# A new calendar for a fused cross-attention and gated self-attention kernel: 119 stretches of 32-column products in place of 144

## What is computed

```
h = x + Wo1 · softmax(q k^T / sqrt(32), 77 context keys, masked) v      # q from layernorm(x), k and v from the context
out = h + svd_moe_o( softmax(q k^T) v )                                 # q, k, v = svd_moe(layernorm(h)), 512 keys
svd_moe(x): x @ Wm + sum over 2 chosen of 8 experts of gate * ((x @ V^T) * S) @ U^T + b
gates: softmax of the top 2 of a small two-layer net on the mean over tokens
```

## Time and profile before

| | us |
|---|---|
| runs | 1422.53, 1434.18, 1422.72 |
| median of the runs | 1422.72 |
| span of the profiled execution, first to last instruction | 1426.7 |
| TensorE busy in it | 1391.0 (97 %) |
| VectorE busy | 951.9 (67 %) |
| ScalarE busy | 861.3 (60 %) |
| GpSimd busy | 679.8 (48 %) |

### The profile page before, as it was taken

The page is one execution under the profiler, slowest core; times in us unless marked ns, Lnnn a source line. Parts: engine busy times, 40 slices in busy tenths (PEclk is TensorE's granted clock), DMA queues, the critical chain, the costliest instruction groups (busy, mean ns, idle before and its releaser), DMA issues.

```text
span 1426.7 us, 17122 instructions
## 1 busy us (share of the span) xinstructions
PE 1391.0 (97%) x5704; PEld 702.4 (49%) x5704; DVE 951.9 (67%) x1687; ACT 861.3 (60%) x1499; POOL 679.8 (48%) x411
## 2 busy tenths in 40 slices
...
PEclk9889999999999999999999999999999999999999
...
GB/s 252 143 53 133 46 68 96 153 76 46 98 110 108 75 54 125 137 61 76 68 111 123 75 59 135 110 85 67 58 104 152 76 46 97 64 101 79 81 39 30
DMA packets 78767, 130.81 MB, mean 92 GB/s; under 512 B 26374, under 2 KB 32134, under 8 KB 75607
## 3 DMA queue, kind: packets, MB, share of 16 engines
...
...
## 4 chain that ended last, share of the span: by engine, by line
PE 85%; ACT 7%; issue 2%; DMA 2%; POOL 2%; DVE 1%; ACTq 0%; SPq 0%; POOLq 0%
PE pj L1217 43%; PE scT L1302 9%; PE sc L1274 8%; PE acc L1331 7%; PE sc L1263 4%; PE pj L1247 2%; PE pj L1311 2%; PE scT L1295 2%; PE pj L1319 2%; PE pj L1340 2%; DMA qs<-shift 2%; PE pj L1190 1%; ACT xhat L810 1%; PE pj L1202 1%; PE pj L1211 1%
## 5 line engine op out<-in xcount | busy, mean ns | idle before, releaser
L925 ACT ACTIVATE probs<-scT 128x512 f32<-128x512 f32 x512 | 288.9, 594 | 303.9 <-PE scT L1302 300.8
L1048 DVE TENSOR_REDUCE negmax<-sc 128x1 f32<-128x512 f32 x512 | 338.0, 684 | 140.7 <-PE sc L1274 139.7
L784 POOL TENSOR_TENSOR probs_sum<-probs_sum,probs 128x1024 f32<-128x1024 f32 x128 | 300.2, 2365 | 57.4 <-ACT probs L925 57.3
L1075 DVE RECIPROCAL inv_sum<-pj 128x128 f32<-128x128 f32 x256 | 225.0, 921 | 59.9 <-PE pj L1340 39.2
L1274 PE MATMUL sc<-ks,qs 96*128 96x512 f32 x512 | 260.1, 541 | 2.4 <-DVE negmax L1048 1.6
L1217 PE MATMUL pj<-XT,Wqk 128*128 128x512 f32 x512 | 257.3, 598 | 0.6 <-DVE Wqk L1140 0.6
L1302 PE MATMUL scT<-qs,ks 99*128 99x512 f32 x512 | 250.9, 517 | 6.2 <-DMA qs<-shift 3.2
L780 POOL TENSOR_TENSOR probs_sum<-probs 128x1024 f32<-128x1024 f32 x64 | 151.4, 2372 | 173.8 <-ACT probs L925 173.8
L790 POOL TENSOR_TENSOR uv_stack<-UVS_sb,uv_stack 96x1024 fp32r<-96x1024 f32 x32 | 75.7, 2367 | 178.1 <-ACT UVS_sb L832 178.1
L1302 PEld LDWEIGHTS scT<-qs,ks 99*128 99x128 f32 x512 | 94.7, 191 | 124.5 <-ACT probs L925 60.4
L754 POOL TENSOR_TENSOR xhat<-xhat,inv_sum 128x128 f32<-128x128 f32 (+1 forms) x56 | 45.1, 806 | 207.7 <-DVE inv_sum L1075 207.7
...
## 6 DMA issues: line engine op xcount, KB each, us to landing
Wqk<-in_WmT SPq DMA_DIRECT2D x16, 1024.0 KB, 6.1
Wvo<-in_WmT SPq DMA_DIRECT2D x16, 1024.0 KB, 6.5
...
X<-in_x SPq DMA_DIRECT2D x8, 1024.0 KB, 6.0
ks<-stage_lo SPq DMA_DIRECT2D x128, 64.0 KB, 2.0
...
```

The costliest lines, as they stand in the source:

```text
L784: nc.gpsimd.tensor_tensor(probs_sum[:, pair], probs_sum[:, pair], probs[:, kt % 2, pair], ALU.add)\
L925: nc.scalar.activation(probs[:, kt % 2, jj, :], scT[:, ST[step], :], ACT.Exp, scale=SCALE)\
L1048: nc.vector.tensor_reduce(negmax[:, 0, n:n + 1], sc[:, SC[step], :], AX.X, ALU.max, negate=True)\
L1075: nc.vector.reciprocal(inv_sum[:, INV[use], at], pj[:, PJ[left_in(full)], at])\
```

## The change

Only the tables change. `PERIOD` goes from 2034 to 32544, which is 16 times 2034, a finer unit for the same period; every number of `CALENDAR` and `OWN` is another. No function changes, the instructions and their sizes are the same ones, and only their order differs. All lines behind the tables stand 23 further down. Two of the lines:

```
-PERIOD = 2034
+PERIOD = 32544
...
-    "normalize": (-1775, 138),
-    "xpose": (-1734, -1732, -1712, -1710, 141, 141, 163, 163),
+    "normalize": (-28358, 2045),
+    "xpose": (-27732, -27691, -27388, -27376, 2393, 2424, 3016, 3035),
```

More of the change, by code:

```diff
@@ L37 @@
 JUNK = 8
-PERIOD = 2034
+PERIOD = 32544
 CALENDAR = {
[L45 to L49, removed]
-    "normalize": (-1775, 138),
-    "xpose": (-1734, -1732, -1712, -1710, 141, 141, 163, 163),
[L52 to L84, removed]
[4 rows of a table removed]
-    "shift": (1339, 1901, 2375, 2899),
-    "shift_move": (1367, 1967, 2390, 2987),
[5 rows of a table removed]
-    "psum": (1569, 1647, 1711, 1722, 1807, 1859, 2147, 2165, 2197, 2257, 2274, 2302, 2564, 2597, 2665, 2695, 2866,
-        2898, 3141, 3176, 3279, 3288, 3326, 3387),
-    "accout": (2115, 2487, 3005, 3448),
-    "den": (1871, 2376, 2959, 3434),
-    "inv": (1895, 1923, 1947, 1965, 2400, 2407, 2409, 2413, 2959, 2961, 2983, 3024, 3444, 3462, 3473, 3476),
-    "divide": (2251, 2923, 3435, 3454, 3559, 3656, 3896),
-    "out2": (3491, 3507, 3522, 3540, 3721, 3723, 3740, 3766, 3789, 3804, 3826, 3889, 3930, 3941, 3958, 3988),
-    "residual2": (3579, 3916, 3925, 4017),
@@ new lines @@
+    "context": (-29912,),
+    "context_v": (-21686,),
+    "load": (-30955,),
+    "stats": (-30467, -30417, -30365, -30353),
+    "deviation": (-29931, 1921),
+    "normalize": (-28358, 2045),
+    "xpose": (-27732, -27691, -27388, -27376, 2393, 2424, 3016, 3035),
+    "q1": (-27018, -26799, -26733, -26633, -26394, -26212, -25732, -24965, -15550, -15396, -14767, -14732, -12279,
+        -11858, -11041, -10500),
+    "q1_split": (-26133, -23568, -13315, -9860),
+    "q1_rows": (-24932, -18086, -12975, -6502),
@@ new lines @@
+    "residual_bias": (14863,),
+    "token_sums": (2676, 3155, 3426, 3514),
+    "gate_hidden": (4094,),
+    "gate_top": (4443,),
+    "gate_scale": (5151,),
+    "uv_hi": (6108, 8121, 10189, 47716),
+    "uv_lo": (6185, 8728, 10473, 50402),
+    "weff": (7069, 7116, 7622, 7869, 9638, 9716, 9943, 9996, 11946, 12201, 12232, 12672, 52772, 53420, 54130, 54572),
+    "qk": (7829, 8195, 8661, 8961, 10075, 10333, 10608, 10898, 18123, 18614, 18740, 18962, 19315, 19542, 19791, 19957,
+        22734, 22871, 23364, 23894, 24917, 25311, 25383, 26567, 34317, 34487, 34893, 35473, 36838, 36970, 37039, 37284),
@@ L119 @@
-    "uv_lo": {(7, 3): 18563, (0, 0): 388, (0, 1): 497, (0, 2): 624, (7, 1): 14786, (7, 2): 14880, (7, 0): 14616},
-    "weff": {(7, 3, 0): 19360, (7, 3, 1): 19558, (7, 3, 2): 19761, (7, 3, 3): 20656, (0, 0, 0): 406, (0, 0, 1): 425,
[12 rows of a table removed]
-    "load": {(0,): -12983},
-    "stats": {(0, 0): -11659, (0, 1): -11047, (0, 2): -9856, (0, 3): -9305},
-    "deviation": {(0, 0): -9177, (0, 1): 86, (7, 1): 14342},
-    "normalize": {(0, 0): -8677, (0, 1): 99, (7, 1): 14377},
-    "xpose": {(0, 0, 0): -8403, (0, 0, 1): -8371, (0, 0, 2): -8329, (0, 0, 3): -8320, (0, 1, 0): 148, (0, 1, 1): 149,
[10 rows of a table removed]
```

147 lines of the change are left out of this document (97 added, 50 removed), and 206 rows, old and new, of tables (CALENDAR, OWN).

## The result

The changed kernel takes 1481.47 us (median of 4 runs, 1472.87 to 1487.37) against 1422.62 before (4 runs): 1.0397 times as long, interval 1.0346 to 1.0448. It is 59 us slower where 9 us less was forecast, and it lies far outside the range. The profiled execution has a span of 1485.6 us, 58.9 more than the one before.

The account below looks back on a forecast made before the run. TensorE's own sequence was taken as the mid-program bound. Stretches -8.5, waits +1.2, start and end -2.0 sum to -9.3 us: 1422.72 to 1413.4 us; range from the terms' bounds 1407 to 1421, overall 1402 to 1425.

Parts of the forecast that it names:

- the stretches: On TensorE, 144 stretches of 32-column products become 119, each saving 0.34 us: -8.5 us.
- the waits in the six periods: TensorE's waits at the transpositions and first `sT` behind the shift: 1.6 us in place of 1.4, six times, +1.2 us.
- start and end: TensorE's gaps at `gate_top(7)`, `shift(7,2)` and `den(7,3)`, with some clock regained: -2.0 us, bounds +1 and -4.
- The wait at the first `sT`: Behind `shift(b,2)`, the period's waits gathered into one piece of 1.6 us for the shift's DMA, not removed.
- my chain: `out1` through `normalize`, `XT` copies and `qk_rows` to the shift's DMA and first `sT`: 29.0 us against TensorE's 27.6.
- the first rival: The 1.4 us wait per period really goes, by an earlier shift landing or shorter chain: 1403.8 us, chance 0.18.
- The third rival: Wq and Wk near the shift make its DMA land after 7.1 us, wait 5.0 per period: 1433.8 us, chance 0.08.
- The clock rival: The granted clock falls behind the gathered wait in all six periods, 1.7 us each: 1423.6 us, chance 0.15.

## Why the prediction was wrong

**What failed first** is the sentence "so there are three terms" (the stretches, the waits in the six periods, start and end). A fourth stood in my own order rows: the loads on SyncE's queue moved, and behind them the ks stack, the qs stack and the qsc stack. I priced the load's new place for the shift alone, and there at 0.2, because that was the wait that I was following, and put the other stacks at nothing without naming what covers them. They cost 16.2, 9.6 and 8.4 us of idle time in the profile after, and the clock fell behind many of these waits. A list of what stands behind each moved load on its queue, and of who waits for that, would have asked for these rows.

**The stretches, -8.5.** The price holds in the new kernel, 0.33 at each stretch, but the 8 us don't show as a whole: with the clock's loss taken off, TensorE's busy time fell by 1363.3 - 1360.7 = 2.6. Part of the difference is that a product behind a wait also counts as busy for longer: the `sc` at 578.97 takes 0.50 to its end, where one behind another product takes 0.23. There are 59 waits above 0.15 after and 42 before; by my estimate, 17 x 0.27 = 4.6. Nor did the 15 stretches joined in the old calendar bring anything: where the order is already tight, a step that is moved brings a wait.

**The wait at the first `sT`, 1.6.** The profile has 1.3 in the period shown. That it is near the forecast is luck, since it is not made as I made it. From the end of `out1` to the first `sT` it takes 31.4 there (586.42 to 617.84), not 29.0. In the period looked at, my chain was no bound: with Wq away the same distance is 29.4, the shift's DMAs have landed by 597.9, and the `sT` starts at 599.95 without a wait. The 1.3 comes from the landing, 6.4 for the later DMA in place of my 3.7, on top of waits and a slow clock in between. So the first rival, that the wait really goes, fits what is seen without Wq, with a landing of 2.9 in place of 3.5, and the load hid it.

**The third rival, the late shift, 0.08 and 1433.8,** named the cause: Wq among the `qk_stack` DMAs. Its landing of 7.1 came nearly true, 6.4, but TensorE was late itself and waited 1.3 for it, not 5.0; the price was for the shift alone and without the clock, and the chance was far too low. What I held against it, a landing of 3.5 "beside such a load already", was the error in reading: the load in the earlier trace rows was not Wq, as I wrote, but Wk, which the old calendar issues behind the ks stack, as the last of its order rows for SyncE shows; in the change Wq stands ahead of it. A landing beside a load that comes behind isn't evidence for one that stands behind a load. The Trainium skill's rule that I weighed (DMA: Bandwidth & Descriptors, Queues, rings and completion order), that a DMA engine takes turns between queues, doesn't protect a small DMA of another queue here: the later DMA of the shift, on ScalarE's queue, landed after 6.4 in the new calendar and 7.5 in the old one with the new loads, against 2.9 to 3.6 in the periods shown without a load ahead.

**The clock rival, 0.15 and 1423.6,** came true as well, on top of the third. It was priced for one gap per period, 10.2; there are several (at `gate_hidden`, at the first `sT` of group 2, at the first `sc` of groups 2 and 3), and the loss is 22 in the profiled executions. I had taken gaps of 0.93 at full clock for safe. Behind 0.62 ahead of `gate_hidden`'s one-column products the clock was 0.66 over 4 us, in four of six periods, and behind 1.02 and 1.64 close together 0.68 over 5; behind 0.90 alone it stayed at 1.00. When it falls is not worked out here.

**Start and end, -2.0.** Nothing: 132.8 and 163.0 against 132.6 and 162.8. At the start that is two changes that happen to cancel: TensorE idles about 5.5 longer in the first 133 us, most of it for `Wvo`, and loses about as much less to the clock (0.92 in place of 0.88). The two waits named in the prediction shrank about as worked out (`gate_top(7)` from 1.01 to 0.2, `shift(7,2)` from 1.90 to 0.35), and about as much came back: 0.99 and 0.92 for the next shift and ks stack, and 3.2 in place of 1.73 at `den(7,3)`.

**The range** was also added up wrongly: its own bounds, -5.1, six times 1.0 and +1, reach 1424.6, not 1421. The result lies far outside either.

**What stays open.** Of the 57 us that the new calendar loses to the old one, Wq's place is about 27 to 29, the q rows and Wvo another 13 or so; the last 15 are many small waits and what the clock takes behind them, which were seen and not taken apart one by one. Why the clock falls behind some gaps and not behind others as long is open too. None of the versions run is faster than the old calendar. Wq on another queue than SyncE's was not tried.
